# A three-layer kernel with a routed FFN on one core: slot lists one tile earlier, the upper plane of x on POOL, h before x

## What is computed

```python
logits = x @ router_weight.T + router_bias                  # 16 experts
top_val, top_idx = jax.lax.top_k(logits, TOP_K)             # 4 of them for each row
gate_up = jnp.einsum('th,ehd->etd', x, gate_up_proj) + gate_up_proj_bias[:, None, :]
gate, up = gate_up[..., ::2], gate_up[..., 1::2]            # 512 of each
glu = jnp.minimum(gate, LIMIT) * jax.nn.sigmoid(gate * ALPHA)
out = jnp.einsum('etd,edh->eth', (jnp.clip(up, -LIMIT, LIMIT) + 1.0) * glu, down_proj) + down_proj_bias[:, None, :]
out = (out * router_scores.T[:, :, None]).sum(axis=0)
```

## Time and profile before

| | us |
|---|---|
| median of three executions | 1051.64 |
| lowest, highest | 1051.58, 1053.58 |
| the profiled execution | 1054.07 |
| its span in the trace | 1052.1 |

### The profile page before, as it was taken

The page is one execution under the profiler, slowest core; times in us unless marked ns, Lnnn a source line. Parts: engine busy times, 40 slices in busy tenths (PEclk is TensorE's granted clock), DMA queues, the critical chain, the costliest instruction groups (busy, mean ns, idle before and its releaser), DMA issues.

```text
span 1052.1 us, 16627 instructions
## 1 busy us (share of the span) xinstructions
PE 807.4 (77%) x3294; PEld 627.6 (60%) x3295; DVE 620.9 (59%) x1137; ACT 437.3 (42%) x732; POOL 310.8 (30%) x352
## 2 busy tenths in 40 slices
PE   4474565688988977778968688788796969788984
PEld 2153355566766756657757566567575757566773
DVE  4788798765565646464636365656565564656452
ACT  4989884233433424242424243444342343333231
POOL 2224577452232311222313122213121212232222
PEclk9665655697999988898989898899998989999998
DMA  8302213547595396788686778978969587944443
GB/s 280 130 1 80 27 55 80 182 110 187 101 173 119 68 161 128 157 131 152 103 154 104 153 111 169 135 167 169 196 104 180 92 122 128 161 95 79 80 81 46
DMA packets 143581, 130.22 MB, mean 124 GB/s; under 512 B 102758, under 2 KB 105062, under 8 KB 143462
## 3 DMA queue, kind: packets, MB, share of 16 engines
q1 hardware_dynamic: 32454, 74.22, 25.1%
q0 software_dynamic: 18416, 36.53, 22.5%
q10 hardware_dynamic: 92592, 18.25, 15.6%
HBM read 84.05 MB, written 28.90 MB: 107 GB/s over the span
## 4 chain that ended last, share of the span: by engine, by line
PE 32%; DMA 23%; issue 8%; DVE 6%; ACTq 3%; ACT 3%; DVEq 2%; POOL 0%; POOLq 0%
PE bank L898 17%; DMA xg<-xn_rows,gslot 16%; PE gate_up_ps L898 14%; DMA gslot<-slot_rows 6%; DVE hl L1095 2%; DVE w L1132 2%; ACT x L646 1%; DVE xl L1085 1%; DMA out_dram<-yb,aslot 1%; PE bank L888 1%; ACTq L263 1%; ACTq L625 1%; ACT sg L668 1%; DVE x L1090 1%; DVEq L263 1%
## 5 line engine op out<-in xcount | busy, mean ns | idle before, releaser
L898 PE MATMUL gate_up_ps<-w,xh 128*128 (+1 forms) x1152 | 368.2, 401 | 0.4 <-DVE xl L1080 0.3
L898 PE MATMUL bank<-w,hh 128*128 (+1 forms) x576 | 220.7, 470 | 136.3 <-DVE hl L1095 134.2
L898 PEld LDWEIGHTS gate_up_ps<-w,xh 128*128 128x128 f32 x1152 | 215.2, 192 | 44.0 <-issue 1.0
L898 PEld LDWEIGHTS bank<-w,hh 128*128 128x128 f32 x576 | 125.6, 227 | 189.4 <-issue 160.1
L452 POOL DMA_INDIRECT out_dram<-yb,aslot x72 | 125.9, 1749 | 367.4 <-ACT yb L675 328.1
L898 PE MATMUL gate_up_ps<-w,xl 128*128 (+1 forms) x576 | 226.9, 394 | 0.0
L1090 DVE SCALAR_TENSOR_TENSOR x<-xg,x 128x512 f16<-128x512 f32 x69 | 47.7, 691 | 244.6 <-ACT x L646 244.6
L443 POOL DMA_INDIRECT xg<-xn_rows,gslot x75 | 81.0, 1080 | 256.5 <-DMA gslot<-slot_rows 158.8
L646 ACT ACTIVATE x<-xg 128x512 f16<-128x512 f32 x69 | 43.5, 631 | 227.3 <-DMA xg<-xn_rows,gslot 144.1
L898 PE MATMUL bank<-w,hl 128*128 (+1 forms) x288 | 130.0, 451 | 0.0
L898 PEld LDWEIGHTS gate_up_ps<-w,xl 128*128 128x128 f32 x576 | 109.8, 191 | 24.5
(11 more groups left out here) (213 smaller groups left out, 804.3 us busy)
## 6 DMA issues: line engine op xcount, KB each, us to landing
raw_w<-_L_ffn_gate_up_proj_dram SPq DMA_DIRECT2D x64, 512.0 KB, 4.4
raw_w<-in_L_ffn_down_proj_dram SPq DMA_DIRECT2D x64, 256.0 KB, 5.4
bgu<-n_gate_up_proj_bias_dram SPq DMA_DIRECT2D x16, 512.0 KB, 12.2
x_sb<-in_x_dram SPq DMA_DIRECT2D x4, 1024.0 KB, 11.2
xn_rows<-xn SPq DMA_DIRECT2D x4, 1024.0 KB, 6.4
out_dram<-x_sb SPq DMA_DIRECT2D x4, 1024.0 KB, 6.7
xg<-xn_rows,gslot POOLq DMA_INDIRECT x75, 4.7
out_dram<-yb,aslot POOLq DMA_INDIRECT x72, 5.0
```

Of the source, the lines that this page charges most:

```text
L898: last = nc.tensor.matmul(out_ps, lhs[:, rows], w[:, bass.ds(buf, 1), part, c, cols].rearrange("p a d -> p (a d)"), start=(m == 0), stop=( ...
```

## The change

Three things change.

- The slot list is loaded one tile earlier: in step T, ACT loads the list of T+4 in place of T+3 (`slots_4` for `slots_3`; the table's helper arrays grow from 5 to 6 entries, and SP loads four lists in front of the loop in place of three).
- The upper fp16 plane of x for T+2 is written by POOL, between the gather of T+3 and the adding DMA of T-1. ACT's multiply is gone.
- On ACT `high_h` now stands ahead of `high_x`, and the early cast of weights ahead of `turn_x`. On DVE the order is `low_h`, `low_x`, `lower_x`, `gate`. TensorE gets a wait for `xh`, since `xl` no longer implies it.

The transposing DMA counts on four semaphores `turned[k]` in place of one.

```diff
             def step(T, k):
                 gather(T + 3, (k + 3) % UNROLL)
+                upper_x(T + 2, (k + 2) % UNROLL)
                 if not known(T):
                     add(T - 1, (k - 1) % UNROLL)
...
+            def upper_x(T, k):
+
+                pool.wait_ge(gathered[k], slot_count(T, k))
+                if not direct(T - 2):
+                    pool.wait_ge(turned[(k - 2) % UNROLL], turn_count(T - 2, (k - 2) % UNROLL))
+                pool.sem_inc(S["turn"], 1)
+                pool.tensor_scalar(x16[:, k % 2, 0:H], xg[:, k, :], X_UNIT, None, ALU.mult).then_inc(S["x16_high"], 1)
...
-                    load_slots(field(act, offs, "slots_3"), (k + 3) % UNROLL, gslot, gslot_in)
-                if not direct(T + 2):
-                    upper_x(T + 2, (k + 2) % UNROLL)
-                if not direct(T + 1):
-                    high_x(T + 1, (k + 1) % UNROLL)
+                    load_slots(field(act, offs, "slots_4"), k, gslot, gslot_in)
                 if not known(T):
                     high_h(T - 1, (k - 1) % UNROLL)
-                if direct(T + 1):
-                    high_x(T + 1, (k + 1) % UNROLL)
+                high_x(T + 1, (k + 1) % UNROLL)
+                if not known(T, FROZEN):
+                    split_high(own, "early")
                 if not direct(T + 2):
                     turn_x(T + 2, (k + 2) % UNROLL)
-                if not known(T, FROZEN):
-                    split_high(own, "early")
...
                 pe.wait_ge(S["lo_done"], need)
+                if not direct(T):
+                    pe.wait_ge(S["xh_done"], T + 1)
                 pe.wait_ge(S["xl_done"], T + 1)
...
+                if not known(T):
+                    low_h(T - 1, (k - 1) % UNROLL)
+                low_x(T + 1, (k + 1) % UNROLL)
                 if not direct(T + 2):
                     lower_x(T + 2, (k + 2) % UNROLL)
-                if not direct(T + 1):
-                    low_x(T + 1, (k + 1) % UNROLL)
-                if not known(T):
-                    low_h(T - 1, (k - 1) % UNROLL)
-                if direct(T + 1):
-                    low_x(T + 1, (k + 1) % UNROLL)
                 gate(T, k, field(dve, own, "bias"))
```

More of the change, by code:

```diff
@@ L225, in xattn_moe_kernel @@
         posk = sb("posk", [P, RT, TOP_K])
-        near = sb("near", [P, 5])
+        near = sb("near", [P, 6])
         turns = sb("turns", [P, 2, E])
@@ L232, in xattn_moe_kernel @@
         spare = hotv[:].rearrange("p r k e -> p (r k e)")
-        past, held = (spare[:, i * 5 * E:(i + 1) * 5 * E].rearrange("p (t e) -> p t e", e=E) for i in range(2))
-        which, block_at = sb("which", [P, 5]), sb("block_at", [P, 5])
+        past, held = (spare[:, i * 6 * E:(i + 1) * 6 * E].rearrange("p (t e) -> p t e", e=E) for i in range(2))
+        which, block_at = sb("which", [P, 6]), sb("block_at", [P, 6])
         move, flag = sb("move", [P, 4]), sb("flag", [P, 8])
@@ L254, in xattn_moe_kernel @@
         gathered = [sem(f"gathered{k}") for k in range(UNROLL)]
+        turned = [sem(f"turned{k}") for k in range(UNROLL)]
         def known(T, below=1):
@@ L347, in _ @@
             sp.wait_ge(S["scat"], 16 * RT * TOP_K * NB)
-            for T in range(1, UNROLL):
-                k = (T + 3) % UNROLL
+            for T in range(UNROLL):
+                k = T
                 sp.wait_ge(gathered[k], 16)
-                tile = field(sp, word(sp, 1, T), "slots_3")
+                tile = field(sp, word(sp, 1, T), "slots_4")
                 sp.dma_start(gslot[:, k, :], slot_d[bass.ds(tile * P, P), :]).then_inc(gslot_in[k], 16)
@@ L1299, in _ @@
             send(V.tensor_reduce(which[:], past, AX.X, ALU.add))
-            link(V.tensor_tensor(held, past, room[:].unsqueeze(1).broadcast_to([P, 5, E]), ALU.mult))
+            link(V.tensor_tensor(held, past, room[:].unsqueeze(1).broadcast_to([P, 6, E]), ALU.mult))
             send(V.tensor_reduce(block_at[:], held, AX.X, ALU.add))
```

34 lines of the change are left out of this document (19 added, 15 removed).

## The result

The changed kernel took **940.25 us** (median; 936.06 to 941.84, 4 runs), the kernel before 1051.66 us (1051.58 to 1053.58, 4 runs). The ratio is 0.893, 95% interval 0.890 to 0.896: 111 us less, where 62 had been forecast. 940 lies at the very end of the predicted range, and by the ratio (939) just outside it. The direction was right, the size was not. Some executions of the kernel before are 2 to 3% longer; medians are of all executions, while ratios, intervals and the times that e8_before_thin and e9_no_pool_thin are set beside leave the longer ones out.

A forecast was written before the change was run, and what follows sets the result against it. TensorE was taken to be bound by waits for `hl` in weight rounds, behind late x. 14 rounds of 4.2 us (59) plus 3 us at the loop's start gave 62 us, so 990 us median, range 940 to 1050.

The forecast's parts named there:

- chain two: Transposing DMA that feeds x, from issue to landing 12.6 us; expected to be what is late next.
- the step that failed: Weight rounds: transposing DMA assumed to take about 12.6 us again, leaving 4.2 us gained in each of 14 rounds.
- the other case (580.3): Weight round: transposing DMA issued at 570.1 lands with the weights at 580.3 instead of at 582.7.
- the two deductions: Taken off a round's gain: 1.3 us for transposes of h waiting for `hb`, 0.9 us for TensorE running slow after waits.
- TensorE's slow spell: TensorE runs slow after long waits in weight rounds: 1.3 and 2.4 us in the rows, 0.9 us still deducted.
- The start of the loop: Down product of tile 2 waits for `hl` behind a gather; moving it up was to gain 3 us of 5.6.
- Casts ahead of the transposing DMA: Two marked steps of each round: the DMA waits for two casts, 2.85 us, and goes 2.4 us later, a price.
- the room: Slack between `hb` and the next transposes of h in a quiet step: 1.7 us, so a multiply up to 2.3 us is free.
- The port: POOL's multiply shares an SBUF port pair with DVE's weight subtractions: 2.4 us in place of 0.65, 3 us lost in all.
- C: Rival: earlier gathers stretch the transposing DMA from 12.6 to 15 us, leaving 17 us gained, 1035 us; chance 0.19.
- D: Rival: POOL's multiply waits up to 3.4 us for DVE in every tile, 75 us lost, 1065 us; chance 0.14.
- B: Rival: all waits for `hl` go and TensorE stays warm, 8 us in each of 14 rounds, 937 us; chance 0.13.

The follow-up runs named there:

- e8_before_thin: Kernel before with weight loads for experts 2 to 15 cut to 16 columns (wrong weights, only time counts): 985.3 us, one execution, ratio 0.926.
- e9_no_pool_thin: Kernel after with the upper plane back on ScalarE and weight loads for experts 2 to 15 cut to 16 columns: 878.9 us, one execution, ratio 0.836.
- e1_slots_only: Kernel before with only the slot lists loaded four tiles ahead; upper plane on ScalarE, x ahead of h: 1030.9 us, ratio 0.964.
- e11_order_act_only: Kernel before with h ahead of x and casts ahead of the transposing DMA on ScalarE only, VectorE in the old order: 1027.4 us, ratio 0.967.
- e14_cast_alone: Kernel before with only the early weight casts moved ahead of the transposing DMA: 1056.7 us, ratio 0.978, no interval.
- e7_gather_late: Kernel after with POOL's gather of tile T+3 moved behind its multiply for T+2: 918.1 us, ratio 0.883 to the kernel before.
- e6_no_order: Kernel after with the old order on ScalarE and VectorE (x ahead of h, casts behind the transposing DMA): 1163.2 us, ratio 1.118 to the kernel before.
- e2_pool_only: Kernel before with only the upper plane's multiply moved to POOL; lists three tiles ahead, x ahead of h: 1345.8 us, ratio 1.260.
- e3_order_only: Kernel before with only the new order (h ahead of x on both engines, casts ahead of the transposing DMA): 920.2 us, ratio 0.862.
- e4_no_slots: Kernel after with the slot lists loaded three tiles ahead again: 1029.8 us, ratio 0.988 to the kernel before.

## Why the prediction was right and wrong

By the ratios the parts add up as: order 1 to 0.865, lists 0.865 to 0.851, POOL 0.851 to 0.893. On 1052 us that is -142, -15 and +44: -113, where the two kernels differ by 111 to 112. The prediction's own sum has a slip that does not matter: 5.3 to 7.7 us, less 1.3 and 0.9, leave 3.1 to 5.5 us a round, not 3.3 to 6.5; the 4.2 taken lies inside either.

**The slot lists.** Right that POOL's waits for them go (5.1 us of 158.8 are left). Wrong that chain two then sets the pace: in the kernel after, engines waited 4.4 us in all for the transposing DMA. The waits of TensorE for `xh` or `xl` at a tile's start, which the prediction had expected, come to 0.3 us. The sum gave the lists no term of their own, and under the new order they earn 15 us. Not foreseen: how much they protect the POOL multiply (0.988 to 0.893), since the list heads a chain that the multiply had just lengthened.

**h ahead of x.** The mechanism is the one that was predicted: `hl` no longer waits for x. VectorE of the kernel before, in the round that the prediction worked out, shows it best:

```profile
594.98 0.69 DVE L1090 SCALAR_TENSOR_TENSOR x<-xg,x 128x512 f16<-128x512 f32 x1 [9.51 <-ACT x L646]
...
595.97 0.69 DVE L1095 TENSOR_TENSOR hl<-bank,hh 128x512 fp32r<-128x512 f32 x1
```

`hl` stands 9.51 us behind a plane of a tile that is needed two steps later. The gain of a round was put too low, and this is **the step that failed**: "the transposing DMA issued at 570.1 lands at 582.7 if it takes 12.6 us again", taken for both marked steps of all 14 rounds. The sum knew of the other case (580.3) and stayed near the long one, since the row had 12.6 us. It doesn't take 12.6 us again, nor the 10.2 us of the short case; the longest landing of the kernel after is 6.6 us. This is what the sum lost by it: had x not been late, the second tile would have started one quiet step of 8.8 us behind the first, at 581.0 + 8.8 = 589.8, and not at 594.6 to 597.0. That is 12.5 us ahead of 602.29, and 10.3 less the two deductions. The round became 10.0 us shorter (31.5 for 41.5 us); over all 14 it is 106.7 / 14 = 7.6 us, with POOL's multiply still in it. Landings of the transposing DMA, least, median and greatest, of the kernel before, the kernel after, e1_slots_only and e11_order_act_only:

```profile
DMA to landing us min/median/max: 3.1/5.0/15.1
```

```profile
DMA to landing us min/median/max: 3.1/4.1/6.6
```

```profile
DMA to landing us min/median/max: 3.5/5.9/13.7
```

```profile
DMA to landing us min/median/max: 3.1/4.4/13.0
```

The bytes and the weight loads are the same in all four. By the transfers' own packets, from the issue to the last of them, 16 of the 69 took over 10 us before, 12 in e1_slots_only, 7 in e11_order_act_only, 12 in e14_cast_alone and 3 in e7_gather_late. In all other runs there are none. The first four have x first on VectorE, the upper plane on ScalarE and full weight loads. The old order alone does not make long landings: e6_no_order and e2_pool_only have it too, with the multiply on POOL, and none takes over 6.3 us; nor does e8_before_thin with thin loads (6.8). So the long landings were no fixed latency of the transfer, but an effect of when and beside what it was sent, and h first on both engines left none in ten kernels and 3 in e7_gather_late. What exactly stretches them is not shown. In the kernel before the transposing DMA is issued within 1 us of the gather of the next tile in 46 of 69 cases (median 0.6 us ahead of it), in the kernel after 3.5 us behind it. But in e3_order_only the distance is 0.5 us and none takes over 10 us, so distance alone is no rule. And landings are not the whole of it: e8_before_thin still waits 73.9 us for `hl`.

**TensorE's slow spell.** Its size was about right. In the rows it cost 1.3 and 2.4 us a round, and the sum kept 0.9 of the 3.7, so it counted on 2.8 us back. The clock gave back 34.8 us of the 106.7, 2.5 us for each of the 14 rounds. Waits for `hl` that are shorter do not rule it out: the one of 1.85 us before 527.64 was still followed by the lower level, from 528.4 on, and 10 such stretches are left of 26.

**The start of the loop.** The sum had 3 us for it and gave no row for its "5.6 us". The two steps in question (from TensorE's transposes of h at 230.57 to those at 263.15 before, 231.85 to 264.36 after) take 32.6 and 32.5 us: nothing was gained.

**Casts ahead of the transposing DMA.** Predicted: a price of 2.4 us a round, 34 us. Measured, with the upper plane on ScalarE: a gain of 60 us (983.5 to 923.1), 4.3 us a round. The step took the queue for what it delays and forgot what it hides: the DMA's issue waits for the lower plane anyway, and the 0.9 us allowed for that were too little once `hl` and `xl` stand ahead of that plane. The prediction also never asked what stands *behind* the issue: `sg`, on which `hb` hangs.

**The multiply on POOL.** Predicted 0.65 us by the nearest row, free up to 2.3 us. Measured 1.49 us at least, 1.53 in the median, 2.13 at most: the length was mis-sized, yet by the prediction's own bound even the longest would have been free. In quiet steps the room was judged rightly (they stay at 8.6 us). It failed in the marked steps: the room was counted along `gate`, `hb` and the transposes of h, and in a marked step the subtractions and `hl` stand behind `gate` on VectorE, with no room. The price is 45 to 57 us. The port is little of it: in e4_no_slots no multiply takes over 1.54 us, and the loss is larger. The order of POOL's queue is part of it (e7_gather_late gets 11 to 22 us back).

**The rivals.** C (pace of the transposing DMA, 1035) fell with the landings. D (held up) did not occur: the multiply takes 2.13 us at most in the kernel after and 2.08 in e6, and the losses of e6 and e2 come from a loop and not from a held multiply. B gave 937 and the result is 940, but that is luck: its waits for `hl` did not all go (49.1 us are left), TensorE was not at full clock throughout, and the multiply, which it had at nothing, cost 45 to 57 us; a gain larger than B's paid for these. Had the multiply been free as forecast, the kernel would have been at 883, outside the range by far.

**The semaphores** and TensorE's wait for `xh` were never taken out, so no run shows what they cost. The prediction had them at nothing.

## What to carry to other kernels

A latency read in a trace belongs to the schedule that it was read in: before it is carried into a new schedule, ask what was in flight beside it and whether that stays. When an instruction that waits (here the issue of a DMA on a compute engine's queue) is moved, price both sides: what it delays, what the wait hides, and what stands behind it. And a chain of waits that runs through a later tile's work into an earlier tile's result, as x into `hl` here, is worth cutting on every engine that it passes: with VectorE left in the old order most of the gain was gone (0.967 against 0.862).

## What the runs showed of the hardware

**POOL's multiply is slow.** 128x512 elements from f32 to f16 take 1.5 us on POOL, against 0.61 us for its cast of 80x512 and 0.63 us for ACT's same work. Of the 69, 18 take about 2.1 us. One of them on POOL of the kernel after, the weight subtraction that runs on VectorE as it begins, and one undisturbed:

```profile
565.75 2.10 POOL L458 TENSOR_SCALAR x<-xg 128x512 f16<-128x512 f32 x1
...
575.32 1.53 POOL L458 TENSOR_SCALAR x<-xg 128x512 f16<-128x512 f32 x1
```

```profile
564.67 1.77 DVE L1143 TENSOR_TENSOR w<-raw_w,w 128x1536 f32 x1
```

The subtraction ends at 566.44, 0.69 us after the multiply began, and the multiply is 0.57 us longer. The other 17 also begin under such a subtraction, 0.7 us before its end, and none of the remaining 51 does. The Trainium skill (page "SBUF — State Buffer", section "SBUF: two separate sides") calls the port pair that the two share an exclusive lock which the first comer holds to the end of its instruction; the trace agrees. The two engines could also just slow each other, and e7_gather_late tells the two apart, since its multiplies begin anywhere from 0.11 to 1.53 us before the subtraction's end: all 23 of them end 1.35 to 1.40 us after it, and so do the 18 here. The longest, with a pair of subtractions beside it of which the first began at 738.62:

```profile
738.84 2.89 POOL L458 TENSOR_SCALAR x<-xg 128x512 f16<-128x512 f32 x1
```

In the kernel after the loss to it is 18 x 0.6 = 11 us, little beside the multiply's own length.

**Issues are stretched too.** POOL's gather takes 1.01 us in quiet steps; in the marked step at 592.19 it took 2.41 us and ended 0.87 us after the subtractions, and the multiply started behind it. Every gather that began under such a subtraction ended 0.86 to 0.92 us after that one's end, with 0.1 to 1.6 us of it still to run:

```profile
592.19 2.41 POOL L449 DMA_INDIRECT xg<-xn_rows,gslot  x1 [0.30 <-issue]
594.67 1.53 POOL L458 TENSOR_SCALAR x<-xg 128x512 f16<-128x512 f32 x1
```

**Landings of one and the same transfer vary with the schedule around it**: 3.1 to 15.1 us for the same transposing DMA in one kernel, 3.1 to 6.6 us in the next, with the same weight loads in both. Weights in flight are part of it, since thin loads bring the first down to 6.2 us at most. What sets it within a round stays open.
